# One transfer moved ahead of a wait on SyncE's queue, in an attention and feed-forward kernel on one core

## What is computed

```
def local_attention(q, k, v):          # windows of 32 tokens
    bk2, bv2 = (look(bk), look(bv))    # each window sees the one before it and itself: 64 keys
    sim = einsum('bhwie,bhwje->bhwij', bq, bk2) * 8.0
    attn = softmax(where(mask, -max, sim))
    out = einsum('bhwij,bhwje->bhwie', attn, bv2)

for i in range(6):
    x = attn_layer(shift_tokens(x), Wqkv[i], ...) + x
    x = ffn_layer(shift_tokens(x), ...) + x
```

## Time and profile before

| what | value |
|---|---|
| median of 3 runs | 3615.62 us (3609.76 to 3617.31) |
| the profiled execution | 3607.98 us, span 3606.2 us |
| PE busy | 3238.4 us, 90% of the span |
| DVE busy | 3119.3 us, 86% |
| ACT busy | 2391.9 us, 66% |
| POOL busy | 2468.9 us, 68% |
| mean granted TensorE clock | 0.980 |
| transfers issued by `bands` | 1344 into PT, 288 into BT, 144 into VT |

### The profile page before, as it was taken

One profiled execution on the slowest core, in us unless ns is written; L12 is line 12 of the kernel. 1 busy time (PEld: TensorE's weight loads), 2 busy tenths in 40 slices (PEclk: granted clock), 3 DMA queues, 4 the chain that ended last, 5 costly groups with the idle time before them and its releaser, 6 DMA issues.

```text
span 3606.2 us, 108351 instructions
## 1 busy us (share of the span) xinstructions
PE 3238.4 (90%) x46108; PEld 2099.0 (58%) x46108; DVE 3119.3 (86%) x2914; ACT 2391.9 (66%) x3945; POOL 2468.9 (68%) x1265
## 2 busy tenths in 40 slices
PE   5658999999999999999989999999999999999986
PEld 3325566666656666656656655666665666665663
DVE  6759989989989989989988998998998998998992
ACT  4645666666666766666666766666666666666664
POOL 4456776777777777767776777777776777776771
PEclk9879999999999999999999999999999999999997
DMA  2001111122111112111121111111211121111111
GB/s 76 1 1 36 39 37 40 37 55 53 38 37 39 41 48 55 40 39 37 36 54 49 42 39 38 40 49 48 48 37 37 38 53 49 44 39 40 37 38 40
DMA packets 150433, 148.32 MB, mean 41 GB/s; under 512 B 39228, under 2 KB 95424, under 8 KB 149952
## 3 DMA queue, kind: packets, MB, share of 16 engines
q1 hardware_dynamic: 149952, 141.39, 15.9%
HBM read 19.62 MB, written 2.10 MB: 6 GB/s over the span
## 4 chain that ended last, share of the span: by engine, by line
PE 48%; DVE 17%; issue 11%; SPq 9%; ACT 4%; DMA 3%; POOL 1%; ACTq 0%; DVEq 0%; POOLq 0%
PE bank L574 15%; PE mid L624 8%; PE bank L673 5%; PE mid L583 5%; PE bank L644 5%; SPq L345 4%; PE mid L611 4%; DMA PT<-PTd 3%; DVE PTd L1384 3%; DVE rot L1411 3%; PE bank L681 3%; DVE rot L1405 3%; PE mid L631 2%; SPq L352 2%; SPq L348 2%
## 5 line engine op out<-in xcount | busy, mean ns | idle before, releaser
L1155 POOL TENSOR_TENSOR swp<-raw,TS 128x1024 f32<-128x1024 f32 x384 | 899.8, 2368 | 823.7 <-DVE raw L1397 823.7
L574 PE MATMUL bank<-wqkv,xs 128*128 128x512 f32 x2304 | 1172.3, 614 | 82.0 <-ACT V L917 63.6
L1145 POOL TENSOR_TENSOR rr<-ssm,nhalf 128x32 f32<-128x32 f32 x192 | 1051.8, 5478 | 16.0
L903 ACT ACTIVATE raw<-bank 128x512 f32<-128x512 f32 x768 | 454.0, 598 | 341.0 <-PE bank L574 273.2
L574 PEld LDWEIGHTS bank<-wqkv,xs 128*128 128x128 f32 x2304 | 380.8, 190 | 366.1 <-issue 206.4
L1391 DVE TENSOR_REDUCE ss<-sq 128x16 f32<-128x1024 f32 x384 | 466.1, 1214 | 47.6 <-ACT sq L911 46.8
L583 PEld LDWEIGHTS mid<-ident,rot 128*128 128x128 f32 x3072 | 354.0, 141 | 225.9 <-issue 163.8
L1411 DVE TENSOR_TENSOR rot<-rot,swp 128x2048 f32<-128x2048 f32 x192 | 440.1, 2292 | 21.1 <-DVE rot L1405 1.4
L1397 DVE TENSOR_TENSOR raw<-raw,rr 128x2048 f32<-128x2048 f32 x192 | 438.0, 2281 | 14.4 <-POOL rr L1145 14.4
L624 PEld LDWEIGHTS mid<-PT,V 128*64 128x64 f32 x6144 | 338.4, 138 | 190.5 <-issue 139.3
L624 PE MATMUL mid<-PT,V 128*64 128x128 f32 x6144 | 382.4, 277 | 69.2 <-DMA PT<-PTd 61.8
(11 more groups left out here) (134 smaller groups left out, 4251.7 us busy)
## 6 DMA issues: line engine op xcount, KB each, us to landing
PT<-PTd SPq DMA_DIRECT2D x1344, 64.0 KB
xs<-F SPq DMA_DIRECT2D x192, 64.0 KB, 1.9
wqkv<-d_wqkv SPq DMA_DIRECT2D x36, 256.0 KB, 3.2
VT<-V SPq DMA_DIRECT2D x144, 64.0 KB
BT<-PTd SPq DMA_DIRECT2D x288, 32.0 KB
fwo<-d_fwo SPq DMA_DIRECT2D x6, 512.0 KB, 5.0
d_out<-X SPq DMA_DIRECT2D x8, 256.0 KB, 2.3
w<-d_w SPq DMA_DIRECT2D x6, 341.0 KB
```

Source lines behind the costliest of these rows:

```text
L574: nc.tensor.matmul(bank[bk][:, :], xs[:, j, :], wqkv[:, c, :], start=True, stop=True)\
L903: nc.scalar.activation(raw[:, j % 2, c * 512:(c + 1) * 512], bank[RAW_BANK[c]][:, :], ACT.Copy)\
L1145: pool.tensor_tensor(rr[:, :], ssm[:, :], nhalf[:, :], ALU.pow).then_inc(rr_ready, 1)
L1155: last = pool.tensor_tensor(dst[:, :, :, t, :], src[:, :, :, 1 - t, :], tab.unsqueeze(2).broadcast_to([P, 2, HEADS, 32]), ALU.mult)
```

## The change

In `bands`, the wait for `pT_ready` is moved from the head of the function to the place behind the transfer into `VT`. The two other waits keep their order.

```diff
             def bands(n, j):
 
-                sp.wait_ge(pT_ready, n + 1)
                 wait(sp, pv_done, n)
                 if j > 0:
                     sp.wait_ge(v_out[1], n)
                     sp.dma_start(VT[P - 2 * W:P - W, :], V[P - W:P, 1 - j % 2, 512:1024]).then_inc(band_moved, 16)
+                sp.wait_ge(pT_ready, n + 1)
                 for w in range(NWIN):
                     r = slice(w * W, (w + 1) * W)
                     sp.dma_start(PT[r, w, :, :], PTd[r, 1, :, :]).then_inc(band_moved, 16)
```

## The result

| | before | with the change |
|---|---|---|
| median | 3613.09 us (4 runs, 3609.76 to 3617.31) | 3569.85 us (4 runs, 3568.91 to 3575.44) |
| ratio | | 0.9883, 95% interval 0.9866 to 0.9900 |
| profiled execution | 3607.98 us | 3569.43 us |

The kernel is 1.2% faster.

What follows compares the result with a forecast made beforehand. One closed loop per batch, crossing SyncE's issue queue at j = 1, was taken to bound the kernel. Gains of 25.3 + 2.5 + 1.2 = 29.0 us led from 3615.6 to 3587 us, range 3573 to 3605 us.

Steps and rivals of the forecast that it cites:

- one loop per batch: Scores, DVE without a gap, turn, ten issues, landing and pv at j = 1, scores: one round takes 69.06 us.
- the cover: SyncE's queue idles ahead of DVE's turn, 1.9 us or more in the steady part, hiding the VT issue's new place.
- The step's size of 0.63 us: Burst behind DVE's turn, j > 0: 0.56 us for the VT issue and gap, 0.07 us for L345 following the wait.
- the base: The median of the runs, 3615.62 us, was taken to lie 7.6 us above the profiled execution, also after the change.
- I take 0.63 us for each, 1.2 us: In the first batch, two more tiles wait over 2 us for their bands; each was to gain 0.63 us.
- 25.3 us: Gain at j = 1 over 45 tiles, capped at PE's idle time: 32 x 0.63 + 5.2 us, passed on whole.
- no rival: TensorE's clock was ruled out as a rival, being granted at 1.00 through a steady batch; no chance given.
- The term for j = 3: Outside the loop, j = 3 counts only where it delays DVE through ACT's squares: 2.5 us taken.
- A: Half the gain: some 0.3 us per round at j = 1, 13 us in all, 3602 us; chance 0.12.
- B: No change: DMA engines set the burst's pace, or VT is not begun earlier; 3615 us, chance 0.09.
- C: Slower: the shifted burst at j = 1 meets stalls and long issues more often; 3630 us, chance 0.04.
- D: More: long issues get rarer at j = 1, up to the whole idle time, 47 us; 3569 us, chance 0.07.

Runs made afterwards that it cites:

- j1_only: The kernel before with the VT transfer ahead of the wait for pT_ready only for tiles with j = 1: 3583.16 us, ratio to before 0.9918.
- extra_j1: The changed kernel with one more VT-kind transfer behind the wait for pT_ready, only at j = 1: 3600.88 us, ratio to before 0.9968.
- extra_j2: The changed kernel with one more VT-kind transfer behind the wait for pT_ready, only at j = 2: 3574.42 us, ratio to before 0.9883.
- two_early: The changed kernel with a second VT-kind transfer ahead of the wait for all tiles with j > 0: 3571.70 us, ratio to before 0.9889.
- first_batch: The kernel before with the VT transfer ahead of the wait only in the first batch's tiles 1, 2 and 3: 3611.35 us, ratio to before 0.9991.
- all_but_first: The VT transfer ahead of the wait in all batches but the first, otherwise the kernel before: 3582.06 us, ratio to before 0.9898.
- split_act: The changed kernel with the last two of the burst's nine transfers at j = 1 issued from ACT's queue: 3558.70 us, ratio to before 0.9852.
- before_again: The kernel before, unedited, measured and profiled once more: 3615.59 us, ratio to before 1.0009.
- j23_only: The kernel before with the VT transfer ahead of the wait only for tiles with j = 2 and 3: 3603.64 us, ratio to before 0.9974.

## Why the prediction was right and wrong

**Right: the loop and the place.** The forecast was one loop per batch that crosses SyncE's queue once, at j = 1. `j1_only` brought the forecast 30 us, `extra_j1` took them back and `extra_j2` did not, and `two_early` showed the cover. The step's size of 0.63 us shows best at j = 2, where long issues are few (5 of 44 tiles in both traces): from the end of the turn to the last issue it took 5.82 us before and 5.20 after. At j = 1 the time from the turn to `pv` fell by 0.62 us (8.60 to 7.98).

**Wrong: the sum.** It came to 3579 us for the profiled execution, which took 3569.4, and to 3587 for the median, which was 3569.85. The 17 us are the 9.6 us by which the sum missed the profiled execution and the 7.6 us of the base, less the 0.4 us by which the median of the changed kernel lies above its profile. The 9.6 us are the start and the rounds with the end.

*The start, 4.0 us.* The step "I take 0.63 us for each, 1.2 us" failed. Up to tile 8 the kernel lost 6.4 us. The sum had 2.4 us there: these 1.2, and another 1.2 for tiles 1 and 5 (0.63 and 0.53), which are among the 45 tiles of its 25.3 us. In the first batch the loop is another one. The feed-forward work is missing, PE waits for the bands in tiles 1, 2 and 3, and DVE waited for ACT's squares behind each of these three `pv` before (2.01, 2.05 and 1.25 us) and behind none after. The loop is one tile long and crosses the queue each time: from `pv` of tile 1 to that of tile 2 it took 17.36 us before and 15.14 after. Of these 2.2 us, 1.2 are the faster `pv` itself (3.21 and 1.97), so the fall of the clock is a good part of the loss. The sign of it stood in a row that I quoted, 3.21 us for `pv` beside 1.97; the idle time of 2.01 us in DVE behind it was in the same trace and not in my rows. I had measured the clock in a steady batch only and wrote that it was no rival. `first_batch` (118.4) and `all_but_first` (124.1) show the start's share of about 6 us in the traces. The runs bound it less well. How it divides between the clock and the shorter bursts was not separated: `j1_only`, which had no fall and moved only tile 1, started in 119.9 us, and `extra_j1` and `split_act` with one fall in 120.3 and 120.0.

*The rounds and the end, 5.6 us.* They gave 30.7 + 1.6 = 32.3 us where 26.7 were forecast (what is left of 25.3 without tiles 1 and 5, and the 2.5). At j = 1 the sum had 0.54 us for each of the 44 rounds, and 0.62 came, 3.5 us more in all. The burst there was 0.69 us shorter and not 0.63, since the long issues weighed a little less too, and the capping at PE's idle time took 0.07 off and not 0.09. The term for j = 3 was 0.08 us per round, 3.6 us, instead of 2.5; against the second profile of before it is 0.17 us per round, over 7 us, so it depends on the execution, of which I had only one sample. The end gave the other 1.1. I had also read over some waits: 13 of the 60 places where PE waits for bands, with 15.2 us, are tiles with j = 3, and the prediction has there "mostly 0.20 us for ACT". After the change there are 4, with 7.5 us.

*The base, 7.6 us.* I went from the profiled execution to the median by adding 7.6 us to both sides. That took the distance for a constant, and it is not one: the profile of before was a light execution, while the profile of the changed kernel lies on its median within 0.4 us. One more run took the median of before itself down to 3613.09, so 2.5 of the 7.6 us were too many from the outset. Against `before_again`, itself a heavy execution, the gain is 0.84 us a round and not 0.70. A typical execution lies between the two, so the change is worth somewhat more than the first profile shows: 42 us by the ratio, against 38.6 in the spans.

**The rivals.** A and B fell with `j1_only`; the issue is real time on the path. C did not occur: the long issues at j = 1 kept their mean excess (0.50 before, 0.47 after). At j = 3 they did get rarer: 42 of the 44 tiles had one before and 32 after, and the burst was 0.97 us shorter there (6.33 to 5.36), not 0.63. With the VT transfer late at j = 3 it is 41 or 42 in all four profiles (`before`, `before_again`, `j1_only`, `first_batch`), and in `j23_only` it is 33. D had the right time (3569 us) by luck and the wrong reason, since it let the long issues vanish at j = 1 and they did not. The range took in only half of D, and it did not add the start, j = 3 and the base, which all err to the same side. Of the tests named for the trace, these came out near the forecast: the wait at L345, bursts shorter by 0.7 us at j = 1, PE's wait at 27 us where "some 30" was said. The round fell by 0.70 us where 0.5 to 0.6 was said. One test did not fit the prediction's own loop. DVE's wait of 3.87 us was to stay unchanged, but DVE's work in a round is the same, so a shorter round must take idle time from it. The mean of that wait fell from 3.84 to 3.62 us, and the wait for ACT's squares behind `pv` at j = 1 from 0.38 to 0.03; the wait of 0.64 stayed.

**The long issues.** The prediction found nothing that makes some issues long, but the traces have it. Beside the kernel's transfers (queue q1) the page of before counts packets of a kind that it calls `instruction`, on queue q8; in the trace each of them has 16 KiB. The first line is the page's (packets, MB, share), the second that of the window from 1527.2 to 1528.2 us, in the tile of the earlier trace rows, and the last two are the two L352 issues of that tile in the chain:

```profile
q8 instruction: 365, 5.98, 0.7%
q8 instruction: 1, 0.02, 5.9%
1527.55 1.00 SPq L352
1528.90 0.63 SPq L352
```

This packet was under way from 1527.22 to 1528.17 us. The issue that began meanwhile took 1.00 us, the next one 0.63. It is so nearly everywhere. Issues by `bands` and `take_x` that took 0.85 us or more coincide with a packet of q8: 138 of 138 in the first profile of before, 140 of 140 in the second, 130 of 130 with the change, and 1574 of 1578 over the twelve traces. They end 0.37 us (median) after the packet has ended. With the packets' times moved by 2 us none of the 138 coincides with one. The other way round, of 131 issues that began while a packet was under way 120 were long. The long ones are not random either: 42 of 44 tiles with j = 3 have one in the first profile, and 5 of 44 with j = 2. So the long issues depend on where a burst stands against these packets. That fits rival C's warning that the change shifts the queue against everything else, and at j = 3 the shift was to the good. Whether the packet itself holds the issue up was not tested by an edit.

**Open.** Why two profiled executions of the kernel before differ by 10 us is not known; the long issues are a part of it. What makes the clock fall in one start and not in another is open too, see below.

## What to carry to other kernels

An issue costs its queue time only where the loop that sets the pace crosses the queue; find that place by asking in which tiles the consumer really waits, then move ahead of the wait everything that does not need what is waited for. Cost the start as a loop of its own, with its own clock, and read durations of the same instruction there and in the steady part side by side. Where runs spread by more than the precision wanted, take a second profile of the kernel before, since one sample can be a light or a heavy one. And where some instructions of a kind are long, lay them beside the `instruction` packets of the DMA queues before you call the cause unknown.

## What the runs showed of the hardware

An issue right behind a semaphore wait took 0.51 us, and one behind another issue 0.59; moving one issue of 0.52 out of the burst therefore saved 0.63 us in all with the gap (5.82 to 5.20 us at j = 2).

Of 131 issues on SyncE's queue that began while an instruction packet of 16 KiB was under way, 120 took 0.85 to 2.02 us instead of 0.59 (first profile of before); nearly every long issue of the twelve traces (1574 of 1578) coincides with such a packet.

The clock in the start: in the four profiles in which `pv` of tile 1 came after 2.05, 2.41, 2.15 and 2.17 us of idle time, it ran at the lower level for a part (3.21 to 3.57 us for 32 matmuls instead of 1.97, with a mean granted clock of 0.79 from 304 to 312 us). Where this idle time was 1.91 us or less, it did not. Yet later tiles went through 2.88 us (before, tile 3), 2.58 us (`j1_only`, tile 2) and 2.32 us (`before_again`, tile 2) at full clock. So the idle time just ahead does not decide by itself, and a stretch with such waits can change its clock from one execution to the next.
